# T = xG and V = xW by seven block products of 256 columns, with the sums on VectorE and GpSimd

## The reference

```
output = x @ weight
alpha  = (x @ wq) @ (x @ wk)^T
alpha  = max(alpha, 0) * (adj != 0);  alpha = softmax(alpha, axis=1)
result = layernorm(x + alpha @ output)
```

## Time and profile before

| | us |
|---|---|
| median of 3 runs | 565.71 |
| lowest, highest | 565.19, 566.07 |
| span of the profiled execution | 564.6 |
| PE busy in it | 552.3 |
| DVE busy | 288.6 |
| ACT busy | 226.8 |
| POOL busy | 18.3 |

### The profile page before, as it was taken

One profiled execution on the slowest core, in us unless ns is written; L12 is line 12 of the kernel. 1 busy time (PEld: TensorE's weight loads), 2 busy tenths in 40 slices (PEclk: granted clock), 3 DMA queues, 4 the chain that ended last, 5 costly groups with the idle time before them and its releaser, 6 DMA issues.

```text
span 564.6 us, 7382 instructions
## 1 busy us (share of the span) xinstructions
PE 552.3 (98%) x2736; PEld 463.7 (82%) x2736; DVE 288.6 (51%) x678; ACT 226.8 (40%) x529; POOL 18.3 (3%) x24
## 2 busy tenths in 40 slices
PE   5999999999999999999999999999999999999995
PEld 4888888888888888888888888888888888888884
DVE  3635555554545445455454555445454554545356
ACT  4534433443434344332543434344343533443153
POOL 0000000000000000000000000000000000000002
PEclk9999999999999999999999999999999999999998
DMA  8902141342504234250343414134250432121003
GB/s 292 377 1 109 66 144 57 113 149 87 176 11 159 92 111 149 74 177 9 115 145 111 149 40 146 74 111 149 74 186 3 147 110 111 74 74 74 0 1 149
DMA packets 23628, 62.03 MB, mean 110 GB/s; under 512 B 1216, under 2 KB 1216, under 8 KB 21696
## 3 DMA queue, kind: packets, MB, share of 16 engines
q1 hardware_dynamic: 23616, 61.87, 31.0%
HBM read 45.09 MB, written 16.78 MB: 110 GB/s over the span
## 4 chain that ended last, share of the span: by engine, by line
PE 97%; DMA 1%; DVE 1%; ACT 0%; POOLq 0%; POOL 0%; issue 0%
PE t_bank L197 11%; PE t_bank L196 11%; PE t_bank L198 11%; PE v_bank L197 10%; PE v_bank L196 10%; PE v_bank L198 10%; PE s_bank L196 6%; PE s_bank L198 6%; PE s_bank L197 6%; PE o_bank L198 5%; PE o_bank L197 5%; PE o_bank L196 5%; PE v_bank L236 1%; PE t_bank L236 1%; DMA xt<-in_x_t 1%; DVE y L474 0%
## 5 line engine op out<-in xcount | busy, mean ns | idle before, releaser
L196 PE MATMUL t_bank<-xt_hi,g_hi 128*128 128x512 f32 x256 | 101.4, 396 | 0.0
L198 PE MATMUL t_bank<-xt_hi,g_lo 128*128 128x512 f32 x256 | 101.3, 396 | 0.0
L197 PE MATMUL t_bank<-xt_lo,g_hi 128*128 128x512 f32 x256 | 101.3, 396 | 0.0
L197 PE MATMUL v_bank<-w_lo,xt_hi 128*128 128x512 f32 x240 | 94.9, 395 | 0.0
L196 PE MATMUL v_bank<-w_hi,xt_hi 128*128 128x512 f32 x240 | 94.9, 395 | 0.0
L198 PE MATMUL v_bank<-w_hi,xt_lo 128*128 128x512 f32 x240 | 94.8, 395 | 0.0
L426 DVE TENSOR_TENSOR t_lo<-t_bank,t_hi 128x512 fp32r<-128x512 f32 x64 | 44.2, 691 | 97.1 <-ACT t_hi L346 97.0
L364 ACT ACTIVATE squares<-y,neg_mean 128x512 f32<-128x512 f32 x64 | 45.5, 712 | 90.6 <-DVE neg_mean L480 87.2
L346 ACT CAST t_hi<-t_bank 128x512 fp32r<-128x512 f32 x64 | 37.5, 586 | 106.9 <-PE t_bank L198 106.9
L426 DVE TENSOR_TENSOR v_lo<-v_bank,v_hi 128x512 fp32r<-128x512 f32 x62 | 42.8, 691 | 70.6 <-ACT v_hi L342 70.6
L342 ACT CAST v_hi<-v_bank 128x512 fp32r<-128x512 f32 x62 | 36.3, 586 | 97.1 <-PE v_bank L198 97.1
(11 more groups left out here) (70 smaller groups left out, 713.1 us busy)
## 6 DMA issues: line engine op xcount, KB each, us to landing
xn<-in_x SPq DMA_DIRECT2D x16, 1024.0 KB, 5.3
xt<-in_x_t SPq DMA_DIRECT2D x15, 1024.0 KB, 7.0
out<-y SPq DMA_DIRECT2D x15, 1024.0 KB, 5.2
adj<-in_adj_t SPq DMA_DIRECT2D x16, 512.0 KB, 3.3
xt<-in_x_t SPq DMA_DIRECT2D x4, 256.0 KB, 5.0
y<-in_w SPq DMA_DIRECT2D x4, 256.0 KB, 5.1
y<-in_wq_t SPq DMA_DIRECT2D x1, 1024.0 KB, 9.0
wk_raw<-in_wk_t SPq DMA_DIRECT2D x1, 1024.0 KB, 11.2
```

Of the source, the lines that this page charges most:

```text
L196: nc.tensor.matmul(dst, a[0], b[0], start=first, stop=False)
L197: nc.tensor.matmul(dst, a[0], b[1], start=False, stop=False)
L198: return nc.tensor.matmul(dst, a[1], b[0], start=False, stop=last)
```

## The change

The core of the diff:

```
+            def t_product(i, slot, at):
+                xh, xl = x_block(i, slot)
+                b = G_ORDER.index(WEIGHT[i])
+                for c in range(2):
+                    cols = slice(c * P, (c + 1) * P)
+                    for k in range(2):
+                        last = add_chunk(ring[at % 4][:, c], (g_hi[:, b, k, cols], g_lo[:, b, k, cols]),
+                                         (xh[:, k], xl[:, k]), k == 0, k == 1)
+                last.then_inc(filled, 1)
...
+            def wait_for_bank(i, m):
+                if i == P3:
+                    pe.wait_ge(copied, m + 1)
+                else:
+                    before = {P1: -PRODUCTS + C22, P6: -PRODUCTS + C12, P5: -PRODUCTS + C11,
+                              P7: -PRODUCTS + C21, P2: U2, P4: U4}[i]
+                    pe.wait_ge(combined, PRODUCTS * m + before + 1)
...
             def fill_o(p, first=False):
                 for g in range(2):
+                    pe.wait_ge(p_lo_ready, R * p + M * g + M)
+                    pe.wait_ge(v_lo_ready, R * p + 3 + g)
                     for n in range(M):
                         if g == 1:
+                            pe.wait_ge(added, R * p + n + 1)
...
@@ ACT @@
+            def step(p, slot, at, more=True, first=False):
+                copy_first(t_matrix(p), at)
+                if more:
+                    for k in range(4):
...
+                            split_a(p + 1, 1 - slot, k)
+                for c in SPLITS:
+                    split_t(p, t_matrix(p), c)
                 for r in range(R):
                     centred_squares(p - 1, 1 - slot, r)
                 exponent(p, 0)
                 exponent(p, 1)
+                copy_first(v_matrix(p), at + PRODUCTS)
                 exponent(p, 2)
                 exponent(p, 3)
+                if more:
+                    split_s(p + 1, S2, None)
+                for r in range(R):
+                    split_p(p, r)
+                if more:
+                    split_s(p + 1, S1, None)
+                    split_s(p + 1, S3, None)
+                split_v(p, C22)
+                if more:
+                    split_s(p + 1, S4, None)
+                split_v(p, C12)
+                split_v(p, C11)
+                split_v(p, C21)
...
+            def combine(m, c, at):
+                product = {U2: P6, U4: P5, U3: P7, C22: P7, C12: P3, C11: P2, C21: P4}[c]
+                dve.wait_ge(filled, PRODUCTS * m + product + 1)
+                before = {U2: None, U4: U2, U3: U2, C22: U4, C12: U4, C11: None, C21: U3}[c]
...
+                nc.vector.tensor_tensor(summed(c), whole, ring[(at + product) % 4][:], op).then_inc(combined, 1)
...
@@ DVE @@
+            def step(p, slot, turn, at):
+                m = t_matrix(p)
+                for c in (U2, U4, U3, C22, C12):
+                    combine(m, c, at)
+                split_t(p, C22)
+                combine(m, C11, at)
+                split_t(p, C12)
+                combine(m, C21, at)
+                split_t(p, C11)
+                residual(p - 1, 1 - slot, before, 0)
+                split_t(p, C21)
+                for r in range(1, R):
+                    residual(p - 1, 1 - slot, before, r)
+                means(p - 1)
                 mask(p, slot, turn, 0)
                 relu_max(p, 0)
                 relu_max(p, 1)
+                variances(p - 1)
                 mask(p, slot, turn, 1)
                 relu_max(p, 2)
                 relu_max(p, 3)
+                for r in range(R):
+                    normalise(p - 1, 1 - slot, r)
+                m, at = v_matrix(p), at + PRODUCTS
+                combine(m, U2, at)
                 invert(p)
+                combine(m, U4, at)
                 for r in range(R):
                     split_p(p, r)
+                for c in (U3, C22, C12):
+                    combine(m, c, at)
+                split_v(p, C22)
+                combine(m, C11, at)
+                split_v(p, C12)
+                combine(m, C21, at)
+                split_v(p, C11)
+                split_v(p, C21)
...
@@ GpSimd @@
+            def step(p, slot):
+                sum_x(p + 1)
+                split_a(p + 1, 1 - slot)
+                reciprocal_root(p - 1)
+                split_s(p + 1)
```

More of the change, by code:

```diff
@@ L29 @@
 EPS = 1e-5
+P1, P6, P5, P7, P3, P2, P4 = range(7)
+PRODUCTS = 7
+U2, U4, U3, C22, C12, C11, C21 = range(7)
+SPLITS = (C22, C12, C11, C21)
+PLACE = {C11: (0, 0), C12: (0, 1), C21: (1, 0), C22: (1, 1)}
+A11, A12, A21, A22 = range(4)
+A_ORDER = (A11, A21, A12, A22)
+S2, S1, S3, S4 = range(4)
+SUM_ORDER = (S1, S2, S3, S4)
+B11, B12, B21, B22, T1, T2, T3, T4 = range(8)
+G_ORDER = (B11, T1, T2, T3, B22, T4, B21)
 def gnn_resnorm(nc: bass.Bass, x, x_t, adj_t, w, wq_t, wk_t, out):
@@ L53, in bank @@
         def bank(name):
-            return ctx.enter_context(nc.psum_tensor(name, [P, 512], F32))
+            return ctx.enter_context(nc.psum_tensor(name, [P, 2, N], F32))
         def sem(name):
             return ctx.enter_context(nc.semaphore(name))
[L60 to L74, removed]
         neg_max = sb("neg_max", [P, R])
@@ L210, in s_chunk @@
[L210 to L219, removed]
@@ L303, in fill_o @@
+                    pe.wait_ge(v_lo_ready, R * p + 3 + g)
                     for n in range(M):
                         if g == 1:
-                            pe.wait_ge(added, R * p + g * M + n - 1)
+                            pe.wait_ge(added, R * p + n + 1)
+                        elif not first:
+                            pe.wait_ge(added, R * p - M + n + 1)
+                        rows = slice(n * P, (n + 1) * P)
                         for m in range(M):
-                            last = o_chunk(g, n, m)
+                            t = g * M + m
+                            last = add_chunk(o_bank[n][:], (p_hi[:, t, rows], p_lo[:, t, rows]),
+                                             (v_hi[:, t], v_lo[:, t]), m == 0, m == M - 1)
@@ new lines, in _, with copy_g @@
+                nc.scalar.copy(wk_hi[:, k], sums[:, k]).then_inc(qk_hi_ready, 1)
+            for s in (S2, S1, S3, S4):
+                act.wait_ge(x_summed, SUM_ORDER.index(s) + 1)
+                nc.scalar.copy(s_hi[:, s], xs[:, s]).then_inc(s_hi_ready, 1)
+            for r in range(R - 1):
+                split_first_v(r)
+            def copy_g(j):
+                act.wait_ge(g_filled, j + 1)
+                nc.scalar.mul(adj[:, j // 2, j % 2::2].bitcast(F32), g_bank[j][:], -1.0).then_inc(g_copied, 1)
@@ new lines, in _ @@
+            split_g(T1)
+            copy_g(2)
+            copy_g(3)
+            split_g(T2)
+            split_first_v(R - 1)
+            split_g(T3)
+            split_g(B22)
+            split_g(T4)
+            split_g(B21)
+            act.wait_ge(filled, P1 + 1)
+            nc.scalar.copy(c1[:], ring[0][:]).then_inc(copied, 1)
+            act.wait_ge(g_filled, K)
+            act.wait_ge(xt_loaded, 16)
+            for k in range(4):
+                nc.scalar.copy(a_hi[:, 1, A_ORDER[k]], xt[:, A_ORDER[k]]).then_inc(a_hi_ready, 1)
@@ new lines, in _ @@
+            split_g(T2)
+            dve.wait_ge(g_summed, 2)
+            sum_g(T4, g_sum(T2), g_block(B21))
+            split_first_v(R - 1)
+            split_g(T3)
+            split_g(B22)
+            split_g(T4)
+            split_g(B21)
+            for c in (U2, U4, U3, C22, C12):
+                combine(0, c, 0)
+            split_t(0, C22)
+            combine(0, C11, 0)
+            split_t(0, C12)
+            combine(0, C21, 0)
+            split_t(0, C11)
+            split_t(0, C21)
```

577 lines of the change are left out of this document (346 added, 231 removed).

## The result

The kernel after runs in **557.05 us** (median of 4 runs, 556.02 to 558.32) against 565.89 (565.19 to 566.42) for the one before in the same session: ratio 0.9847, 95% interval 0.9831 to 0.9862. It is 8.8 us faster, where 536.0 was predicted: the sign is right, and 70% of the expected gain is missing. The profiled executions have spans of 564.6 and 556.4, a gain of 8.2. Here and in all later runs, executions with a lowered clock throughout, or more than 1.5% longer than the fastest of their kernel, are left out.

The account below looks back on a forecast made before the run. PE was taken as the bound (busy 98%). Span 564.6 - 34.1 + 1.2 + 0.5 + 2.2 = 534.4, plus 1.1 to the runs' median, 535.5, rounded to 536 us; own range 531 to 542, 8 in 10 from 522 to 572.

Parts of the forecast that it names:

- Step 1: T and V on PE: seven products, 84 matmuls of 256 columns at 120 ns, 10.06 us a matrix; -34.1 us.
- The far end of 109 ns: Matmul spacing at 256 columns by the Trainium skill's rule; at 108 ns at best, 43 us better.
- Step 2: DVE's sums in the loop: 24.3 of 31.34 us a pair, all waits met, so costed at nothing.
- 0.3 us slacks: Spare time in T before PE's third and fourth O outputs, which wait for DVE's first and second residuals.
- Rival A: DVE and GpSimd hold each other up at low parts of v and t: 568 to 592 us; 20%.
- rival B: The same hold-up in part, or late sums: slacks fail by 0.5 to 1.5 us a pair, 543 to 558; 20%.
- step 6: The start: +1.2 us from G's sums and low parts on DVE, +0.5 from pair 1's late copy.
- Step 3: ACT's added copies and casts: 17.2 us a pair, 55%, costing nothing.
- step 5: SP's four transfers per pair, the x load waiting for the store: hidden, costing nothing.
- Step 4: GpSimd's 12 operations per pair at 1.3 us each: 16.6 of 31.34 us, the bound only above 2.5 us each.
- Step 7: The end: the last O needs C11 and C12 of V, +2.2 us.

Follow-up runs that it names:

- e7: The kernel before with nine small declarations reordered so every large tile begins on a multiple of 256 bytes, no seven products: 555.78 us.
- e6: The kernel after with the tiles of g and w moved to 32 bytes past a multiple of 256: 556.17 us.
- e1: The kernel after with GpSimd's sums of x and low parts in the loop (pairs 1 to 14) cut to 1 of 512 elements: 544.0 us.
- e4: The kernel after with DVE taking the first two residuals ahead of the last two low parts of T, nothing left out: 546.27 us.
- e3: The kernel after with GpSimd's sums and low parts in the start cut to 1 of 512 elements, loop unchanged: 546.6 us.
- e11: e10 with GpSimd making pair 2's sums and low parts before w's low parts, and pair 0's reciprocal root earlier: 537.8 us.
- e2: The kernel after with GpSimd's twelve operations per pair in the loop (pairs 1 to 14) replaced by memsets that read nothing: 544.11 us.
- e10: The kernel after with a reordered start, C11's low part ahead of C21 in T(0) and last V, e4's order and e6's shift: 541.24 us.
- e5: The kernel after with all large tiles beginning 128 bytes past a multiple of 256: 558.0 us.

## Why the prediction was wrong in size

The prediction summed to 534.4 of span and the profile has 556.4, 22.0 more. By its steps:

- **Step 1, seven products: right.** 120 ns a matmul and 10.08 a matrix (predicted 10.06). Of the 34.1 us, though, 9.6 could be had without the seven products, by lining up the tiles alone (e7), which the text treated only as the condition for 120. The far end of 109 ns did not come, and lining up T and V was not what made 120 either: e6 has 118 without it.
- **Step 2, the sums on DVE at nothing: the step that failed.** "All waits are met" rested on low parts of 691 ns, from a row with one input in PSUM and GpSimd idle. Both inputs in SBUF change nothing by themselves (683 for `xt_lo`, 688 in e1); with GpSimd reading beside them they take 1084 to 1228, and the two 0.3 us slacks named there fail by 0.84 a pair: 13 x 0.84 = 10.9 of the 22.0. The place was the one named (the third and fourth O output). e1 and e4 show the cause from two sides. Rival A had the mechanism: a low part behind a combination is spaced 1.10 (0.49 more than 0.61), one behind another 1.70. It had the price too high: the eight low parts are longer by 4 x (1.23 - 0.69) + 4 x (1.08 - 0.69) = 3.7 a pair, not 5.4, and 0.84 of that reached PE. So the loop came out as rival B, the same contention in part, 0.84 a pair within its 0.5 to 1.5. That the time lies in B's range is luck in part: 535.5 + 10.9 is 546.4, and the other 11 are step 6's, which B did not have.
- **Step 3 and step 5, ACT and SP at nothing: right.** No row shows PE waiting for a cast or a load in the loop.
- **Step 4, GpSimd: right alone** (1.29 against 1.3), wrong in company (1.6 to 1.75). The ratio of 1.96 in the Trainium skill (GPSIMD Engine Reference, 3.1 Elementwise), measured there at 2048 elements, had given an estimated 1.35 with DVE's row; the trace has 1.29.
- **Step 6, the start at +1.2 and +0.5: failed**, by 8.0 before T(1) and 3.5 in pair 1, so 11.5, more than the loop. It priced G's low parts at 0.69, and most took 1.75 to 1.78; it didn't price DVE's queue ahead of U2 with GpSimd active (four `p_lo` in 5.52 us); and it had no term for the clock, 1.3 us each in S(0) and T(1). e3 shows that GpSimd's work is behind all of it: without it pair 2 starts at 81.40 instead of 93.35, and the prediction had 81.9 (48.87 + 1.2 + 31.34 + 0.5).
- **Step 7, the end at +2.2: right**, 1.84. This is the 0.3 that the sum gets back: 10.9 + 8.0 + 3.5 - 0.3 = 22.1.

What stays open: why 32 bytes between the operands of a matmul cost 6 ns at 512 columns and save 2 at 256; and whether the waits and the lower clock that e11 still has in the start (3.0 us at T(0)'s end, 1.6 in S(0), 5.1 in O(0)) can be had back by yet another order. Neither was tried further.

## What to carry to other kernels

Before work is given to GpSimd, list the DVE operations that will run beside it and have both inputs in SBUF. Here each came to 1.10 to 1.70 us instead of 0.61. So leave one input in PSUM, or put whatever PE waits for ahead of them. A slack of 0.3 us is no slack when a new engine starts up next to it. And split a change into its free parts first: here the reordered declarations alone had the whole gain, and two residuals moved ahead of two low parts (e4) were worth 10.8 us more.

## What the runs showed of the hardware

- DVE with two SBUF inputs beside GpSimd reading SBUF (128x512 each): one such operation behind another, both advance in lock step at 1.70 us, where alone they take 0.69 and 1.29 (issued every 1.25); behind a combination the low part is spaced 1.10. Four `p_lo` take 5.52 and 5.07 (after, e11) instead of 1.66. With one input in PSUM DVE keeps its 0.68. GpSimd's writing (memset, 0.52) disturbs nothing (e2). In one place (e10) four normalisations, with one tile in SBUF as input, took 2.85 instead of 1.92 beside one low part on GpSimd; no run tests that by itself.
- Where operands lie matters by the size of the matmul: 233 ns with a 32 byte offset against 227 without at 512 columns (e7), 118 with against 120 without at 256 (e6). 128 or 0 past a multiple of 256 is the same (e5).
- The clock can fall behind a wait of PE within a busy stream: to the 1.2 GHz level for 2.7 us behind 2.2 us in T(1) of the kernel after, beginning 1.3 us later (213 ns a matmul of 256 columns instead of 120), and for 3.6 us behind 3.3 us in O(0) of e11 (granted 0.50 and 0.55 in the windows above). Behind e10's 5.0 us in V(1) it fell at once, for 3.3 us, and so it did in S(0) of e1 behind 3.8 us, for 21 matmuls. It doesn't behind each: the 2.2 us of e1 in T(0), the 1.84 at the end and the 0.35 in the loop had no such sequel.
